# FP4 rounding of 66 tiles: the add and the subtract move from GpSimd to VectorE

## The reference

```python
def nvfp4_qdq(x, select_num):
    D = x.shape[-1]
    s = jnp.maximum(jnp.max(jnp.abs(x)) / (448.0 * 6.0), 1e-12)
    xb = (x / s).reshape(x.shape[:-1] + (D // BLOCK, BLOCK))
    sb = jnp.clip(jnp.max(jnp.abs(xb), axis=-1, keepdims=True) / 6.0, 1e-12, 448.0)
    a = xb / sb
    q = jnp.sign(a) * FP4_LEVELS[jnp.digitize(jnp.abs(a), FP4_BOUNDS)]
    dq = (q * sb).reshape(x.shape) * s
    ...
xq = nvfp4_qdq(x2[:, up_reorder_index], SEL_UP)
wg = nvfp4_qdq(w_gate[:, up_reorder_index], SEL_UP)
wu = nvfp4_qdq(w_up[:, up_reorder_index], SEL_UP)
h = jax.nn.silu(xq @ wg.T) * (xq @ wu.T)
hq = nvfp4_qdq(h[:, down_reorder_index], SEL_DOWN)
wd = nvfp4_qdq(w_down[:, down_reorder_index], SEL_DOWN)
out = hq @ wd.T * mlp_output_scale + x2 @ lr_A @ lr_B
```

## Time and profile before

| what | value |
|---|---|
| median of 3 runs | 952.35 us (951.04 to 953.06) |
| the profiled execution | 955.64 us, span of its trace 954.3 us |
| PE busy | 759.9 us (80%) |
| DVE busy | 691.8 us (72%), 1195 instructions |
| ACT busy | 335.0 us (35%) |
| POOL busy | 352.5 us (37%), 296 instructions |
| mean granted TensorE clock | 0.91 |
| chain that ended last | DVE 40%, PE 38%, issue 9%, ACT 6%, DMA 4%, POOL 2% |

### The profile page before, as it was taken

The page is one execution under the profiler, slowest core; times in us unless marked ns, Lnnn a source line. Parts: engine busy times, 40 slices in busy tenths (PEclk is TensorE's granted clock), DMA queues, the critical chain, the costliest instruction groups (busy, mean ns, idle before and its releaser), DMA issues.

```text
span 954.3 us, 11830 instructions
## 1 busy us (share of the span) xinstructions
PE 759.9 (80%) x4300; PEld 552.2 (58%) x4300; DVE 691.8 (72%) x1195; ACT 335.0 (35%) x443; POOL 352.5 (37%) x296
## 2 busy tenths in 40 slices
PE   0878746867859998889987878938689999938887
PEld 0644422635647765666655656727468788926665
DVE  4677865556387899799999998674566332399996
ACT  3655666334263444335444421124222111121111
POOL 1001312011363564645646555312244100036775
PEclk9998976888898999999999998968779999978999
DMA  8432357588445555555545420113011111110000
GB/s 286 149 100 100 131 172 209 171 256 253 143 157 156 177 188 185 169 163 188 184 158 181 136 66 32 37 37 88 12 55 45 31 45 31 34 31 11 23 23 34
DMA packets 56042, 110.82 MB, mean 116 GB/s; under 512 B 9889, under 2 KB 20673, under 8 KB 55985
## 3 DMA queue, kind: packets, MB, share of 16 engines
q1 hardware_dynamic: 42560, 78.68, 25.8%
q10 hardware_dynamic: 9040, 17.30, 5.4%
q0 software_dynamic: 4384, 14.09, 5.0%
HBM read 91.89 MB, written 18.15 MB: 115 GB/s over the span
## 4 chain that ended last, share of the span: by engine, by line
DVE 40%; PE 38%; issue 9%; ACT 6%; DMA 4%; POOL 2%; SPq 1%; ACTq 0%; DVEq 0%; POOLq 0%
PE bank L1016 10%; PE bank L1017 9%; PE bank L1018 9%; DVE q_m L1515 4%; DVE hot L1619 4%; DVE hot L1621 3%; DVE x L1724 2%; PE bank L1113 2%; DVE q_c L1500 2%; ACT hot L1383 2%; DVE q_a L1791 2%; DVE wsum L1636 2%; DVE q_a L1682 2%; DVE q_r L1678 1%; DVE q_d L1701 1%
## 5 line engine op out<-in xcount | busy, mean ns | idle before, releaser
L1383 ACT ACTIVATE hot<-rep,levels 128x2048 f16<-128x2048 f16 x58 | 121.4, 2093 | 56.4 <-PE bank L1113 49.3
L1874 POOL TENSOR_TENSOR w_l<-wsum,w_h 128x512 fp32r<-128x512 f32 x46 | 60.9, 1324 | 209.1 <-ACT w_h L1392 209.1
L1846 POOL TENSOR_TENSOR q_a<-q_a,q_m 128x384 f32<-128x384 f32 (+3 forms) x66 | 78.7, 1193 | 103.4 <-DVE q_m L1518 103.1
L1016 PE MATMUL bank<-zt_h,w_h 128*128 128x512 f32 (+1 forms) x232 | 96.9, 418 | 17.5 <-DVE x L1724 12.2
L1113 PE MATMUL bank<-hot,diag 128*32 128x512 f16 x1392 | 96.2, 416 | 3.7 <-DVE q_d L1643 3.7
L1017 PE MATMUL bank<-zt_l,w_h 128*128 128x512 f32 (+1 forms) x232 | 93.5, 403 | 0.0
L1018 PE MATMUL bank<-zt_h,w_l 128*128 128x512 f32 (+1 forms) x232 | 93.0, 401 | 0.0
L1849 POOL TENSOR_TENSOR q_a<-q_a,q_m 128x384 f32<-128x384 f32 (+3 forms) x66 | 78.6, 1191 | 5.2
L1016 PE MATMUL bank<-w_h,xq_h 128*128 128x512 f32 (+1 forms) x192 | 73.3, 382 | 1.7 <-DVE w_l L1740 1.7
L1018 PE MATMUL bank<-w_h,xq_l 128*128 128x512 f32 (+1 forms) x192 | 71.5, 373 | 0.0
L1017 PE MATMUL bank<-w_l,xq_h 128*128 128x512 f32 (+1 forms) x192 | 71.5, 373 | 0.0
(11 more groups left out here) (195 smaller groups left out, 1788.3 us busy)
## 6 DMA issues: line engine op xcount, KB each, us to landing
rep<-codes SPq DMA_DIRECT2D x58, 512.0 KB, 4.6
codes<-c SPq DMA_DIRECT2D x29, 256.0 KB, 3.5
raw<-in_codes_gu_t ACTq DMA_DIRECT2D x14, 512.0 KB, 4.6
sc<-in_scales_gu_t SPq DMA_DIRECT2D x56, 128.0 KB, 3.1
raw<-in_codes_attn_t ACTq DMA_DIRECT2D x8, 512.0 KB, 4.0
raw<-in_codes_down_t ACTq DMA_DIRECT2D x7, 512.0 KB, 3.9
sc<-in_scales_down_t SPq DMA_DIRECT2D x28, 128.0 KB, 3.8
wide_buf<-in_gate_flat SPq DMA_DIRECT2D x5, 512.0 KB, 5.2
```

The lines of the kernel that those rows point to most:

```text
L1016: PE.matmul(psum, lh, rh, start=first, stop=False, **kw)
L1383: S.activation(hots[plan.slot[hot_ring(t), (t, m)]][:], codes_in_place(t), ACT.Relu, bias=levels[:, RISES:RISES + 1], scale=levels[:, RISE ...
L1846: G.tensor_tensor(ua[:, 0:nq], ua[:, 0:nq], um[:, 0:nq], ALU.add).then_inc(own.sem, 1)
L1874: G.tensor_tensor(wl[:, k, :], wsum[t % 2][:], wh[:, k, :], ALU.subtract).then_inc(sem("made_pool"), 1)
```

## The change

VectorE does the whole of the rounding. The bits instruction joins another constant, so that its result is already the large number; the maximum with the smallest large number is folded into the add and into the subtract, each a `scalar_tensor_tensor` of two SBUF tensors. The subtract leaves the negative of the rounded value, and the finish, now a `scalar_tensor_tensor` too, multiplies by -1. GpSimd's two instructions are gone, and with them the delay of one item between rounding and finish: the finish stands in the plan right behind the rounding of its own item.

```diff
@@ make_plan, fp4_weights @@
-        pending = None
...
+                finish((name, c, o))
                 yield
-                if pending:
-                    finish(pending)
-                pending = (name, c, o)
                 yield
-        finish(pending)
@@ turned_tiles @@
-        staged = turned = None
-        for item in [*items, None, None]:
+        turned = None
+        for item in [*items, None]:
...
-            if staged:
-                p.add("qturn", *staged)
-                turn4(staged, ("dve", "take", *staged))
+                p.add("qturn", *item)
+                turn4(item, ("dve", "take", *item))
...
-            turned, staged = staged, item
+            turned = item
@@
-        if step >= 3:
+        if step >= 2:
             next(first_hidden)
@@ dve_program @@
-        def magic(ua, um, nq):
...
-            steady.up(V.tensor_scalar(um[:, 0:nq].bitcast(U32), ua[:, 0:nq].bitcast(U32), 0x7F800000, 0x00400000,
-                                      ALU.bitwise_and, ALU.bitwise_or))
+        def round_off(ua, um, nq):
...
+            u, m = ua[:, 0:nq], um[:, 0:nq]
+            steady.up(V.tensor_scalar(m.bitcast(U32), u.bitcast(U32), 0x7F800000, 0x0B400000, ALU.bitwise_and,
+                                      ALU.bitwise_or))
             steady.wait_ge()
-            return V.tensor_scalar(um[:, 0:nq], um[:, 0:nq], 1.5, 2.0 ** 22, ALU.max, ALU.mult)
+            steady.up(V.scalar_tensor_tensor(u, m, 1.5 * 2.0 ** 22, u, ALU.max, ALU.add))
+            steady.wait_ge()
+            return V.scalar_tensor_tensor(u, m, 1.5 * 2.0 ** 22, u, ALU.max, ALU.subtract)
@@ wfinish @@
-                dve.wait_ge(*done("pool", "wround", *key))
+                dve.wait_ge(*done("dve", "wround", *key))
...
-                V.tensor_tensor(blocks_of(q_out[plan.slot["q_out", ("w", *key)]][0:orow, :], nq), blocks_of(ua, nq),
-                                spread_of(cc[:, 0:nq // FP4_BLOCK], orow, nq), ALU.mult).then_inc(
-                                    sem("wfinish_dve"), 1)
+                V.scalar_tensor_tensor(blocks_of(q_out[plan.slot["q_out", ("w", *key)]][0:orow, :], nq),
+                                       blocks_of(ua, nq), -1.0, spread_of(cc[:, 0:nq // FP4_BLOCK], orow, nq),
+                                       ALU.mult, ALU.mult).then_inc(sem("wfinish_dve"), 1)
@@ pool_program @@
-            elif kind == "wround":
...
-            elif kind == "round":
```

More of the change, by code:

```diff
@@ L1688, in dve_program @@
                     steady.wait_ge()
-                magic(ua, um, nq).then_inc(sem("wround_dve"), 1)
+                round_off(ua, um, nq).then_inc(sem("wround_dve"), 1)
                 if nq < w:
@@ L1792, in dve_program @@
                 steady.wait_ge()
-                magic(ua, um, nq).then_inc(sem("round_dve"), 1)
+                round_off(ua, um, nq).then_inc(sem("round_dve"), 1)
             elif kind == "qturn":
@@ L1796, in dve_program @@
                 ua = q_tmp[plan.slot["q_tmp", key]][0]
-                dve.wait_ge(*done("pool", "round", *key))
+                dve.wait_ge(*done("dve", "round", *key))
                 for m in vacant("q_out", key):
                     dve.wait_ge(*m)
-                V.tensor_tensor(blocks_of(q_out[plan.slot["q_out", key]], nq), blocks_of(ua, nq),
-                                spread_of(c, P, nq), ALU.mult).then_inc(sem("qturn_dve"), 1)
+                V.scalar_tensor_tensor(blocks_of(q_out[plan.slot["q_out", key]], nq), blocks_of(ua, nq), -1.0,
+                                       spread_of(c, P, nq), ALU.mult, ALU.mult).then_inc(sem("qturn_dve"), 1)
             elif kind == "take":
@@ L1841, in gather @@
                 dma_sem(key), 16)
-        def round_off(ua, um, nq, sem_in, own):
-            pool.wait_ge(*sem_in)
-            G.tensor_tensor(ua[:, 0:nq], ua[:, 0:nq], um[:, 0:nq], ALU.add).then_inc(own.sem, 1)
-            own.n += 1
-            own.wait_ge()
-            return G.tensor_tensor(ua[:, 0:nq], ua[:, 0:nq], um[:, 0:nq], ALU.subtract)
-        own = Steady(pool, sem("pool_steady"))
         for step in plan.steps:
@@ L1897, in pool_program @@
                                ("gather", *key))
-            elif kind == "wround":
-                orow, w, nq = wround_size(*key)
-                ua, um, _, _ = (v[0:orow, :] for v in q_tmp[plan.slot["q_tmp", ("w", *key)]])
-                round_off(ua, um, nq, done("dve", "wround", *key), own).then_inc(sem("wround_pool"), 1)
             elif kind == "gu_mul":
@@ L1927, in pool_program @@
                                        bass.bass_isa.ReduceOp.max).then_inc(sem(kind + "_pool"), 1)
-            elif kind == "round":
-                _, _, nq, _, _ = fp4_source(key)
-                ua, um, _, _ = q_tmp[plan.slot["q_tmp", key]]
-                round_off(ua, um, nq, done("dve", "round", *key), own).then_inc(sem("round_pool"), 1)
             elif kind == "fin":
```

## The result

The changed kernel takes **976.19 us** in the median of 4 runs (971.81 to 978.73), the kernel before 952.7 (951.04 to 954.08) beside it. The ratio is 1.0242, 95% interval 1.0201 to 1.0284: slower. The forecast of 965.3 has the sign, and the measured time lies in its range of 951 to 980; the growth is 23.5 us where 13 was forecast.

A forecast was written before the change was run, and what follows sets the result against it. VectorE bounds the full stretch (252 of 271 us busy) and the last stage. Terms +6 (20 - 17 + 4 - 1), +4, +4.5 and -1.5 sum to +13 us: 965.3 us forecast, range 951 to 980.

The forecast's parts named there:

- the rival of a dear form: Everywhere: a `scalar_tensor_tensor` from SBUF costs more than the plain form; at +0.1 us each, 980 us; 6 in 100.
- Relief, -17, and +4 for the subtractions that stay: Full stretch (295 to 566 us): 17 us less standing behind GpSimd's rounding, 4 more behind its remaining subtractions.
- The rival that wanted 28 of relief: Full stretch: all 28 us of standing beside L1500's belong to rounding and go; 950 us, faster; 12 in 100.
- the one in which GpSimd's subtractions cost it all back: Full stretch: remaining GpSimd subtractions cost VectorE 45 us instead of 25; 985 us, 10 in 100, as many for 975.
- the one that hides the added work: Where TensorE's products set the pace, VectorE's +6 and +4 vanish; 955.4 us; 15 in 100.
- VectorE's idle time, -1: Full stretch: VectorE's own 19 idle us take about 1 us of the added time back.
- a longer stretch that VectorE does not fill: Sign that would show the prediction wrong: the stretch gets longer without VectorE being busy throughout; no size given.
- Stores on SP: what it has queued behind is needed more than 10 us later: SP's queue: FP4 tiles stored one step earlier; SP waits for the finish, but the loads behind are not needed soon.
- 566 to 630 us, +4: Last 8 weight tiles: 6.5 us added, some 1 of standing gone, idle time hides some; +4 us.
- The tiles before 295 us, at nothing: Two weight tiles before the full stretch, beside longer idle times: no cost; without that cover, 2 x 0.78 us.
- x stage, +4.5: x tiles and first hidden products: +4.5 us, including TensorE standing 3.3 us for the fourth x tile.
- Last stage, -1.5: h tiles: 2.9 us added and 3.9 of standing gone per token tile, 1.1 back; -1.5 us together.

The follow-up runs named there:

- late_w: The change with the weights' finish and store put back to one item later, as before: 964.54 us, ratio 1.0118 to the kernel before.
- half_w: late_w with the subtraction of the constant moved one item later too, to the finish: 959.87 us, ratio 1.0048 to the kernel before.
- h_only: Only the 24 h items rounded on VectorE and finished at once, weights and x tiles as in the kernel before: 951.58 us, ratio 0.9979.
- h_fin: h_only with the last addition to `x` moved from GpSimd to VectorE too: 948.54 us, ratio 0.9935 to the kernel before.
- late_store: The change with only SP's store of each weight tile one item later, VectorE's order untouched: 972.75 us, ratio 1.0207 to the kernel before.
- mid_w: The change with a weight tile's finish and store later, in late_w's VectorE slot but for its own item: 967.25 us, ratio 1.0139.

## Why the prediction was right, and where it was wrong

*What bounds the kernel, and the price of the new form.* Right. A `scalar_tensor_tensor` from SBUF takes 559 ns at 384 columns and 692 at 512, as the plain form does; the rival of a dear form falls. VectorE's timeline in the last stage has the distances:

```profile
898.11 0.69 DVE L1516 SCALAR_TENSOR_TENSOR q_a<-q_m,q_a 128x512 f32<-128x512 f32 x1
898.84 0.69 DVE L1518 SCALAR_TENSOR_TENSOR q_a<-q_m,q_a 128x512 f32<-128x512 f32 x1
...
903.33 0.69 DVE L1800 SCALAR_TENSOR_TENSOR q_d<-q_a,blk 128x512 f32<-128x512 f32 x1
903.94 0.68 DVE L1806 TENSOR_TENSOR zt_l<-bank,zt_h 128x512 fp32r<-128x512 f32 x1
```

A dependent successor starts after 0.73 us, an independent one after 0.61. The Trainium skill (VectorE: DVE Perf Modes, "The DRAIN you can't avoid") found no such difference between eight copies with a semaphore after each and eight with one after the last. These rows differ by 0.12 us, and they decide, as in the prediction.

*Relief, -17, and +4 for the subtractions that stay.* Right together, within 4 us. Adding up what each VectorE instruction of the full stretch takes beyond the fastest of its operation, tiles and shape in any of the traces gives 54.2 us of standing before and 37.4 in the change: 16.8 less, where the two terms make 13. Put down to the GpSimd instruction that each overlaps longest, 20.0 us were rounding's, a relief 3 us larger than forecast, and the rest grew from 34.2 to 37.4, nearly the +4. The reason that I gave for the +4 is doubtful, though: between the 23rd and the 47th `wsum` the rest is 31.7 us before and 33.8 in the change, but 32.4 in late_w and 31.5 in half_w, whose instructions are as long. The rival that wanted 28 of relief and the one in which GpSimd's subtractions cost it all back both fall, and so does the one that hides the added work.

*VectorE's idle time, -1, and with it "the finish's place at nothing".* **This is the step that failed.** The prediction has no term for the place of a weight tile's finish: it let idle time give 1 us back, and idle time in the full stretch grew by 11.5 instead (19.0 to 30.5). So one of its own signs of being wrong came, "a longer stretch that VectorE does not fill". I had counted the finish as an instruction that keeps its price wherever it stands. late_w shows what the place costs, 11.7 us. With the weights' finish left where it was the kernel takes 964.5, and the forecast was 965.3; that agreement is partly luck: in its profiled execution late_w is only 3.7 us late at the end of the weights, where 10 were forecast, and its x stage costs 7.9 instead of 4.5.

*"Stores on SP: what it has queued behind is needed more than 10 us later".* Wrong, and worth 3.4 us by medians whose intervals overlap. The distance from issue to use of the `rep` broadcasts, 8.5 us or more before, falls to between 4 and 7 in places, and three of them are waited for.

*566 to 630 us, +4.* Between 549 and 636 us the change lost 5.2 (late_w 3.1). About right, with the place's part on top.

*The tiles before 295 us, at nothing.* Open. At the 23rd `wsum` the eight kernels whose weights finish later or are unchanged stand between -4.6 and +1.0 us against the profile of before, the four with the early finish between +1.0 and +5.7. But h_only and h_fin run the same instructions as the kernel before up to there, and stand at -4.6 and -1.3: one profiled execution each can't part this. It also bears on the 11.7 us, which are whole programs: at the end of the weights the trace of late_w is 14.0 us ahead of the change's, and 6.4 of that it had at the 23rd `wsum`.

*x stage, +4.5.* Mechanism right, the sum 3 us low. The stall for the fourth x tile is 3.42 us where 3.3 was worked out, in TensorE's timeline of the change:

```profile
727.30 0.39 PE L1013 MATMUL bank<-w_h,w_l 64*128 64x512 f32 x1
731.11 0.66 PE L1279 MATMUL bank<-ident_r,q_d 128*128 128x128 f32 x4 [3.42 <-DVE q_d L1800]
```

The first product starts at 719.01, 0.8 us earlier against the end of the weights than before (forecast: 1). The second is 23.3 late, so 5.6 for the whole. Some 1.4 of that are the clock, which I had named and not priced: behind the stall seven matmuls, from 732.11 on, start 0.43 us apart, where the second product of the kernel before has 0.23. The other 2 us are the clock too. Two later stretches that answer to each other, in the kernel before and in the change:

```profile
753.00:762.00 9.00, 7.27 (x36) 5.81 (x35) 2.26 (x4) 1.19 (x2) 0.96 (x1) 1.00 0.10 29
```

```profile
777.00:787.00 10.00, 8.11 (x33) 6.40 (x32) 2.56 (x4) 1.67 (x3) 1.89 (x2) 0.83 0.16 46
```

Behind a wait for `w_l` of about the same length in both, the product of the change runs its first matmuls, from the second to the eighth, at 0.63 us each, at the lower of the clock's two levels (1.2 GHz), where the kernel before has 0.40: a granted clock of 0.83 against 1.00. Before, that product's end is 8.0 us behind the one ahead of it, in the change 10.1. These 2 us do not come with every such kernel. half_w and late_store have the same waits of TensorE in the x stage, 3.42 and 1.89 us, and keep the upper level there (half_w below); their x stages cost 6.1 and 5.9. late_w and mid_w lose the 2 us as the change does.

```profile
755.00:766.00 11.00, 9.11 (x44) 7.29 (x43) 2.57 (x4) 2.01 (x4) 1.89 (x2) 1.00 0.15 42
```

*Last stage, -1.5.* Measured -2.7, with a token tile of 11.68 us in the forecast's 11.5 to 12.

So the sum of 13 lacks 7.7 us in the weights, for want of a term for the place of finish and store, and 3.2 in the x stage, about what the clock cost there; 1.2 came back in the last stage. That 976 still lies in the range is partly luck: its upper part was kept for a dear form and for GpSimd's subtractions, and neither came.

## What to carry to other kernels

When work moves onto a full engine, look at what else the edit moves: an operation that used to fill the wait for another engine, and now follows directly on its producer, lengthens the piece in which the engine serves no one else. Here that cost 11.7 us, about as much as the forecast had charged for the whole change. Price each instruction that is brought forward by who stands behind it, in every queue, the DMA queue's waits among them; and try the arithmetic and its place apart, since here the arithmetic was nearly free.

## What the runs showed of the hardware

- A GpSimd instruction can cost VectorE time without VectorE waiting for it: leaving out 132 two-tensor GpSimd instructions, and none of VectorE's, made the program 27.6 us shorter. GpSimd was busy for only 37% of the span, and the profile of the kernel before has one wait of VectorE for it, 1.7 us.
- A store that waits for its tile holds back the loads behind it on the same queue: SP waited 46 us more for finishes and 41 us less for `wsum`, and the shortest distance from a `rep` broadcast to its use in the full stretch fell from 8.5 to 4.1 us. With the stores alone put back the program was 3.4 us shorter by medians, which is not clear of noise.
- A wait of TensorE of 1.73 us left the clock at its upper level in the kernel before. In the change the same wait, 1.89 us, is followed by seven matmuls 0.43 us apart instead of 0.23; a stall of 3.42 us lay 48 us ahead of it. That stall is not enough as a cause: half_w and late_store have both waits to the hundredth, and the clock stays up.
